# The causal mask under the row maxima: a masked maximum on DVE in place of identity products on PE

## What is computed

```python
scores = jnp.einsum('bhqd,bhkd->bhqk', q, k) * scale
causal = jnp.tril(jnp.ones((T, T), dtype=bool))
scores = jnp.where(causal, scores, -jnp.inf)
attn = jax.nn.softmax(scores, axis=-1)
out = jnp.einsum('bhqk,bhkd->bhqd', attn, v)
```

## Time and profile before

| what | value |
|---|---|
| median of 3 runs | 613.81 us (613.73 to 614.38) |
| the profiled execution | 617.44 us, its span 615.7 us, mean granted PE clock 0.955 |
| PE / PE weight load busy | 549.5 us (89%) / 255.0 us |
| DVE busy | 416.2 us (68%) |
| ACT busy | 350.7 us (57%) |
| POOL busy | 157.3 us (26%) |
| row maxima on DVE, L1604 | 480 instructions, 279.9 us |

### The profile page before, as it was taken

The page is one execution under the profiler, slowest core; times in us unless marked ns, Lnnn a source line. Parts: engine busy times, 40 slices in busy tenths (PEclk is TensorE's granted clock), DMA queues, the critical chain, the costliest instruction groups (busy, mean ns, idle before and its releaser), DMA issues.

```text
span 615.7 us, 10700 instructions
## 1 busy us (share of the span) xinstructions
PE 549.5 (89%) x3869; PEld 255.0 (41%) x3885; DVE 416.2 (68%) x1063; ACT 350.7 (57%) x673; POOL 157.3 (26%) x217
## 2 busy tenths in 40 slices
PE   6577799888899988898989999999999999999993
PEld 3323234434433333332333334543545445347662
DVE  4396989768888869786878887776666721643144
ACT  4413267754765767745767776656556666653330
POOL 9631012353534155342111221301101102201000
PEclk9877899997999999996989999999999999999998
DMA  3992023005022001020010101001000000010000
GB/s 117 178 210 91 21 70 104 2 1 200 17 71 62 1 25 56 26 79 28 2 54 2 53 2 54 2 2 53 2 3 2 1 2 1 2 35 2 0 15 20
DMA packets 27846, 25.64 MB, mean 42 GB/s; under 512 B 7377, under 2 KB 24401, under 8 KB 27538
## 3 DMA queue, kind: packets, MB, share of 16 engines
q1 hardware_dynamic: 27410, 24.17, 14.4%
q0 software_dynamic: 384, 0.79, 0.7%
HBM read 17.30 MB, written 7.34 MB: 40 GB/s over the span
## 4 chain that ended last, share of the span: by engine, by line
PE 69%; DVE 8%; SPq 8%; ACT 7%; DMA 3%; issue 3%; POOL 1%; DVEq 0%; ACTq 0%; POOLq 0%
PE ps L1227 15%; PE ps L1210 12%; PE ps L1306 10%; PE ps L1362 10%; PE ps L1189 9%; ACT pr L1382 5%; DVE mparts L1604 4%; SPq L913 4%; PE ps L1292 3%; SPq L967 2%; PE ps L1286 2%; DMA qs<-nparts 2%; PE ps L1238 2%; PE ps L1267 2%; PE ps L1184 1%
## 5 line engine op out<-in xcount | busy, mean ns | idle before, releaser
L1382 ACT ACTIVATE pr<-ps 128x512 f32<-128x512 f32 (+1 forms) x480 | 249.9, 554 | 167.1 <-PE ps L1210 137.0
L1604 DVE TENSOR_REDUCE mparts<-ps 128x1 f32<-128x512 f32 (+3 forms) x480 | 279.9, 630 | 89.1 <-PE ps L1189 87.5
L1210 PE MATMUL ps<-qs,ks 64*128 64x512 bf16 (+7 forms) x560 | 153.3, 338 | 18.3 <-ACT pr L1382 10.1
L1189 PE MATMUL ps<-ks,qs 61*128 61x512 bf16 (+7 forms) x576 | 155.4, 347 | 6.9 <-DMA qs<-nparts 3.7
L1227 PE MATMUL ps<-pr,vs 128*32 128x512 f32 (+3 forms) x1152 | 125.0, 507 | 1.5 <-ACT pr L1382 0.3
L1083 POOL TENSOR_SCALAR_AFFINE_SELECT pr<-pr 128x512 f32<-128x512 f32 x96 | 60.9, 634 | 227.7 <-ACT pr L1382 227.6
L1210 PEld LDWEIGHTS ps<-qs,ks 64*128 64x128 bf16 (+1 forms) x576 | 44.6, 96 | 136.9 <-ACT pr L1382 97.5
L1306 PE MATMUL ps<-w,work 128*128 128x128 f32 x512 | 67.7, 283 | 0.0
L1189 PEld LDWEIGHTS ps<-ks,qs 61*128 61x128 bf16 (+1 forms) x576 | 51.0, 100 | 37.8 <-DVE mparts L1604 19.6
L1362 PE MATMUL ps<-feat,w 128*128 128x512 f32 x128 | 65.8, 621 | 0.0
L1306 PEld LDWEIGHTS ps<-w,work 128*128 128x128 f32 x512 | 60.2, 191 | 9.5 <-issue 9.3
(11 more groups left out here) (138 smaller groups left out, 501.3 us busy)
## 6 DMA issues: line engine op xcount, KB each, us to landing
qs<-scr0q SPq DMA_DIRECT2D x48, 64.0 KB, 2.3
qs<-scr1q SPq DMA_DIRECT2D x84, 32.0 KB
ks<-scr1k SPq DMA_DIRECT2D x84, 32.0 KB
ks<-scr0k SPq DMA_DIRECT2D x36, 64.0 KB, 2.2
scr0q<-parts SPq DMA_DIRECT2D x4, 384.0 KB, 2.9
scr0k<-parts SPq DMA_DIRECT2D x4, 384.0 KB, 3.8
scr1q<-parts SPq DMA_DIRECT2D x4, 384.0 KB, 2.6
scr1k<-parts SPq DMA_DIRECT2D x4, 384.0 KB, 2.6
```

The lines of the kernel that those rows point to most:

```text
L1189: last = pe.matmul(bank[:, h, :], queries(F, 0, h0 + h, i * P, P), keys(F, 0, h0 + h, 512 * c, w), start=not diagonal, stop=True, skip_gro ...
L1210: last = pe.matmul(to[:, h, :], keys(F, 3, h0 + h, j * P, P), queries(F, 3, h0 + h, qb * 512 + lo, n), start=True, stop=True)
L1382: act.activation(pr[:, st % PSLOTS, h0:h0 + nh, 0:STEPS[st][3]], scores_at(F, v), ACT.Exp, scale=GROUPS[F][0].scale).then_inc(exped, 1)
L1604: dve.tensor_reduce(mparts[:, F % SLOTS, h0:h0 + nh, i, c], maxes_at(F, u), AX_X, ALU.max).then_inc(taken, 1)
```

## The change

PE no longer lays down a mask. `maxima` issues only the score products. On DVE a unit that is not diagonal is reduced as before; a diagonal one takes one `tensor_tensor_reduce` a head: it adds a row table `cmask`, [128, 512] bf16 with zeros and in its last 128 columns the mask, to the scores, writes the sum back to the same bank, and gives its maximum. The tables `identb`, `identx`, `cmaskx` and the step `halves` go. The planner's costs are changed with it. POOL's counter `made` ends at 9 in place of 10, and PE starts when it is 1, not 3.

```diff
     if kind == "max":
         i, c, _, nh, w = MAXES[step[2]]
-        masked = (512 * c + w == (i + 1) * P) * nh * (128 if GROUPS[step[1]][0].n == 0 else 192)
-        return [(PE, (masked + nh * w) / 2400 + 0.01 * nh), (DVE, 0.1 + nh * w / 880)]
+        reads = nh if 512 * c + w == (i + 1) * P else 1
+        return [(PE, nh * w / 2400 + 0.01 * nh), (DVE, 0.1 * reads + nh * w / 880)]
...
-        identb = sb("identb", [P, P], BF16)
-        identx = sb("identx", [P, P], BF16)
-        cmask = sb("cmask", [P, 2, P], BF16)
-        cmaskx = sb("cmaskx", [P, 2, P], BF16)
+        cmask = sb("cmask", [P, 512], BF16)
...
+            pool.memset(cmask[:, :], 0.0).then_inc(gchain, 1)
...
+            pool.affine_select(out=cmask[:, 512 - P:512], in_=cmask[:, 512 - P:512], compare_op=ALU.is_ge, fill=NEG,
+                               base=0, pattern=[[-1, P]], channel_multiplier=1).then_inc(made, 1)
...
-                diagonal = 512 * c + w == (i + 1) * P
-                if diagonal and GROUPS[F][0].n == 0:
-                    pe.matmul(bank[:, :, w - P:w], identb[:, :], cmask[:, 0:nh, :], start=True, stop=False,
-                              skip_group_check=True)
-                elif diagonal:
-
-                    own = slice(HALF * (h0 // 2), HALF * (h0 // 2) + HALF)
-                    low, high = ((identb, cmask), (identx, cmaskx))[::-1 if h0 // 2 else 1]
-                    pe.matmul(bank[:, :, w - P:w], low[0][own, :], low[1][own, 0:nh, :], start=True, stop=False,
-                              skip_group_check=True)
-                    pe.matmul(bank[:, :, w - HALF:w], high[0][own, :], high[1][own, 0:nh, HALF:P], start=False, stop=False,
-                              skip_group_check=True)
                 for h in range(nh):
                     last = pe.matmul(bank[:, h, :], queries(F, 0, h0 + h, i * P, P),
                                      keys(F, 0, h0 + h, 512 * c, w),
-                                     start=not diagonal, stop=True, skip_group_check=True)
+                                     start=True, stop=True)
...
-                    dve.tensor_reduce(mparts[:, F % SLOTS, h0:h0 + nh, i, c], maxes_at(F, u),
-                                      AX_X, ALU.max).then_inc(taken, 1)
+                    bank, to = maxes_at(F, u), mparts[:, F % SLOTS, h0:h0 + nh, i, c]
+                    if 512 * c + w < (i + 1) * P:
+                        last = dve.tensor_reduce(to, bank, AX_X, ALU.max)
+                    else:
+                        for h in range(nh):
+                            last = dve.tensor_tensor_reduce(bank[:, h, :], bank[:, h, :], cmask[:, 512 - w:512], 1.0, -3.0e38,
+                                                            ALU.add, ALU.max, to[:, h:h + 1])
+                    last.then_inc(taken, 1)
```

More of the change, by code:

```diff
@@ L262, in wanted @@
     add("loads", [(F - 0.5, ("copy_v", F)) for F in range(NF)])
-    add("once", [(0.05, ("weights",)), (1.1, ("b2_parts",)), (1.05, ("partners",)), (1.2, ("halves",)), (1.5, ("moe_weights",)),
+    add("once", [(0.05, ("weights",)), (1.1, ("b2_parts",)), (1.05, ("partners",)), (1.5, ("moe_weights",)),
                  (-1.99, ("pads", 0)), (-1.98, ("pads", 1)), (-0.62, ("pads", 2)), (NF + 0.9, ("quiet",))])
@@ L279 @@
 OWN_LANE |= {kind: kind for kind in ("hidden", "relu", "expert", "pick_up", "x1", "x12", "scores", "pv", "mask", "copy_v", "quiet",
-                                     "pads", "ones", "halves", "weights", "moe_weights", "b2_parts", "partners")}
+                                     "pads", "ones", "weights", "moe_weights", "b2_parts", "partners")}
 def lane(stream, step):
@@ L319 @@
          "relu": (ACTE, 0.6), "expert": (PE, 1.15), "pick_up": (DVE, 1.4), "layer_norm": (DVE, 1.4), "out": (SP, 0.5),
-         "copy_v": (POOL, 0.66), "pads": (POOL, 3.6), "ones": (POOL, 4.0), "halves": (POOL, 1.7), "weights": (SP, 5.2), "moe_weights": (SP, 1.1),
+         "copy_v": (POOL, 0.66), "pads": (POOL, 3.6), "ones": (POOL, 4.0), "weights": (SP, 5.2), "moe_weights": (SP, 1.1),
          "partners": (POOL, 2.4), "quiet": (PE, 0.0)}
@@ L415, in needs @@
         out = [("load", F, k, h) for k in range(2) for h in ((0, 1) if half is True else (int(half),))]
-        return out + [("pads", F)] * (F < SLOTS) + [("halves",)] * (F == ATT[0].groups)
+        return out + [("pads", F)] * (F < SLOTS)
     if kind == "combine":
@@ L1032, in pads @@
                 pool.wait_ge(done["pads"], 2 * nth("pads", slot))
-            def halves():
-                pool.wait_ge(*before)
-                pool.memset(identx[:, :], 0.0).then_inc(gchain, 1)
-                pool.memset(cmaskx[:, :, :], 0.0).then_inc(gchain, 1)
-                pool.wait_ge(gchain, 5)
-                for first, base in ((0, HALF), (HALF, 0)):
-                    part = slice(first, first + HALF)
-                    pool.affine_select(out=identx[part, :], in_=identx[part, :], compare_op=ALU.not_equal, fill=1.0,
-                                       base=base, pattern=[[-1, P]], channel_multiplier=1).then_inc(done["halves"], 1)
-                    pool.affine_select(out=cmaskx[part, :, :], in_=cmaskx[part, :, :], compare_op=ALU.is_ge, fill=NEG,
-                                       base=base, pattern=[[0, 2], [-1, P]], channel_multiplier=1).then_inc(done["halves"], 1)
-                pool.wait_ge(done["halves"], 4)
             def partners():
@@ L1092, in _ @@
                     pads(*args)
-                elif kind == "halves":
-                    halves()
-                    before[:] = [done["halves"], 4]
-                    continue
                 elif kind == "partners":
```

31 lines of the change are left out of this document (12 added, 19 removed).

## The result

| | before | changed |
|---|---|---|
| median, us (4 runs each) | 614.04 | 622.43 |
| its runs, us | 613.73 to 614.38 | 621.2 to 622.76 |
| profiled execution, us | 617.44 | 622.16 |
| its span, us | 615.7 | 620.2 |
| mean granted clock of it | 0.955 | 0.924 |

The ratio is 1.0126, with a 95% interval of 1.0096 to 1.0156: slower by 1.3%, which is 7.7 us by the ratio and 8.4 us between the medians. The forecast was 619 us in a range of 604 to 632. The first lines are the page of the changed kernel, busy time by engine and the chain's shares, which answer to the earlier trace rows.

A forecast was written before the change was run, and what follows sets the result against it. PE was taken as last nearly everywhere, beside a DVE some 80% full; 15.5 us lost on DVE less 10.0 gained on PE gave +5.5 us, 619 us from the 613.8 median, in a range of 604 to 632.

The forecast's parts named there:

- the likeliest case, 616 to 625 us: The forecast's own case, around 619 us, slower by 0.9%; chance 0.36.
- Where the bound lies: PE nearly everywhere last, DVE some 80% full sharing a three-bank ring; DVE late at 50 to 90 us, PE alone 374 to 500.
- The gain, 10.0 us: Removed PE mask products: 4.0 us from 90 to 280, 1.4 from 280 to 374, 4.6 from 374 to 500.
- The chain share of 15.7 us: The mask products' share of the chain over the four stretches from 50 to 500 us, together 15.7 us.
- 374 to 500: all 4.6 us: Beside expert products, the masks' whole 4.6 us chain share comes back, PE being the bound.
- The loss, 15.5 us: Of 34.6 us added DVE time, paid: 4.1 us from 50 to 90, 6.2 to 280, 4.2 to 374, 1.0 to 500.
- the cheap bound: Each masked maximum's second DVE instruction costs 0.073 us, 28.0 us for 384; the dear bound was 74.9 us.
- The order of steps stays nearly as it was, so I add nothing for it.: The planner's step order was taken as nearly unchanged by the new unit costs, and costed at nothing.
- absorbed: Rival: DVE's slack absorbs the addition after 90 us, 9.2 us faster, 605 us (603 to 611); chance 0.36.
- Dear: Rival: the second DVE instruction takes 0.195 us a step, about 27 us slower, 641 us; chance 0.09.
- PE loses its clock: Rival: PE, with fewer products and more waits, gets the lower clock; 6.8 us on top, 626 us; chance 0.07.
- the signs I named: DVE busy up 25 to 45 us, masked maxima within 20 ns of reductions, last maxima later, stretch after 500 us unchanged.

The follow-up runs named there:

- e4: The change for groups 9 to 11 alone, in the order of the kernel before; 614.28 us, ratio 0.9985 to the kernel before.
- e2: PE part alone, old order: no mask products, plain reductions for all units, first-pass mask left out; 610.12 us, ratio 0.9930 to the kernel before.
- e3: DVE part alone, old order: mask products stay on PE, diagonal units take the masked maximum with zeros; 621.65 us, ratio 1.0124 to the kernel before.
- e8: The kernel before's instructions in the order the planner made for the change; 627.87 us, ratio 1.0206 to the kernel before.
- e10: The kernel before with only the transposes and rows of groups 1, 3, 6 and 7 moved to about the new order's places; 621.79 us, ratio 1.0098.
- e1: The change's instructions in exactly the step order of the kernel before; 617.52 us, ratio 1.0035 to the kernel before.
- e11: The change, planned with a group's maxima done in 0.85 of a group's length instead of 0.9; 613.06 us, ratio 0.9971 to the kernel before.
- e12: The kernel before's instructions, planned with maxima done in 0.85 of a group's length instead of 0.9; 606.89 us, ratio 0.9886 to the kernel before.
- e6: The change in the old order, mask products also kept on PE for groups 0 to 2; 617.19 us, ratio 1.0024 to the kernel before.
- e9: Old order, plain reductions everywhere, mask products only for groups 0 to 2; 613.70 us, ratio 0.9973 to the kernel before.

## Why the prediction was right, and where its steps were not

The time fell into the likeliest case, 616 to 625 us, on the forecast's side. That is in part luck: the gain was 5.7 us too large, the loss 7.9 us too large, and a term stood at nothing that is worth 6 to 7 us; together the three errors leave about 4.

- **Where the bound lies.** Held in the main. DVE was the late engine of the ring more often. Beside the expert products it still has 29.5 of 126 us idle, where it had 39.6; yet e4 shows that even there the change returns little.
- **The gain, 10.0 us.** Measured 4.3 (e2). The chain share of 15.7 us (which leaves out 226 to 280 us, where the mask products hold another 1.1 us of the chain) is near the 13.6 us by which PE's busy time fell in e2, and the 14 us by which its work fell at full clock (587 to 573). What failed is that part of it was to turn into waits and nothing into clock: PE with fewer products was granted 0.939 instead of 0.955. In the bookkeeping at full clock that is 573/0.939 - 573/0.955 = 10 us given back; by the slopes of 184 to 679 us per unit it is 3 to 11. How the 10 us divide between waits and clock is not shown. The term "374 to 500: all 4.6 us", less the 1.0 paid there, is 3.6 us net; e4 allows 2.4 at most.
- **The loss, 15.5 us.** Measured 7.6 (e3). The count was right, and so was the choice of the cheap bound, but the step was 0.05 us instead of 0.073: 24.7 us of DVE time in the changed kernel instead of 34.6. That brings 15.5 to 11.1; the rest must lie in the shares that I took as paid, which no run measures one by one.
- **"The order of steps stays nearly as it was, so I add nothing for it."** This step failed outright: it stood at nothing, with no row behind it. The planner's costs of a maxima unit changed, at least 538 of 1888 steps moved, and the rows of four groups left one to four score units later. With the old instructions that is 12.7 us (e8), of which 6 by those rows alone (e10); with the change's it is 6 to 7 us (e1 against the change). The moves could be seen in the two lists, and I priced them by two short cuts of them, not by what waits for a group's rows.
- **Sum by measured terms:** 7.6 - 4.3 + (6 to 7) = 9 to 10 us, against 7.7 and 9.4 by the two ratios measured.

Of the rivals, *absorbed* is out for the order as it is; in a better one the change comes out 0.3% under the old kernel (e11), but 0.9% over the old instructions planned the same way (e12). *Dear* fell with the timeline: 0.05 us, not 0.195. *PE loses its clock*, which I gave 0.07, is also what the profile shows: 0.955 to 0.924. It came together with the forecast's own terms and not on top of them, and it belonged in the sum. How much of a lower clock is a cause of the lost time, and how much is only the mark of waits that cost time anyway, stays open: of the two attempts to raise it by more products, e6 raised it by 0.008 and left the time, and e9 left it and cost 0.4% against e2.

Of the signs I named, DVE busy came out just under its 25 us, the masked maximum 27 ns over a reduction of the same width rather than within 20, and the maxima end at 497.4 us instead of 494.4. The stretch behind them is 122.8 us long instead of 121.3, so 1.5 us of the 4.5 between the two spans are lost there.

## What to carry to other kernels

Moving work from a nearly full PE to a DVE that is 80% full lost in two orders of three. Read the chain share of what goes, and then ask what the clock will do with the holes. Where a planner sets the order, measure the change in the old order too, and the old instructions in the new one: here the same instructions in three orders lie 3.2% apart (0.9886 to 1.0206), more than the change itself does in any of them. And price a moved step by who waits for it, not by how far it moved.

## What the runs showed of the hardware that was not expected

- A masked maximum is two instructions on DVE, and the small one, 139 ns in its row, costs about 0.05 us: it starts at 317.42 us, 0.08 us before the row of the first ends, and the next masked maximum starts at the same moment. By the Trainium skill (VectorE: DVE Perf Modes, section Two Vector instructions with no wait between them) the accumulator read is held only where its output starts in another quadrant of partitions than the last one did; both start at partition 0 here. The trace agrees: it starts before the row in front of it has ended.
- Reading a bf16 table beside PSUM and writing the result back to PSUM costs no rate here: 1.02 ns a column, against 1.035 for a reduction that writes one.
- The granted clock fell when PE was emptied, when DVE was made later, and when the steps moved: 0.955 before, 0.939 without the masks (e2), 0.947 with DVE's pairs and all masks (e3), 0.933 with both (e1), 0.922 to 0.925 for both in the new order, 0.941 for the old instructions there (e8), 0.963 for them in e12's order. The Trainium skill (TensorE: Matmul & The Clock Gate, Part 1: The HAM clock gate) has the rule that a less busy PE is granted the lower clock. Most of these runs go that way; e9's added products left it at 0.939, and e8 has the lower clock with a PE idle for no longer than before.
